# Tile-by-tile masks before the first attention, two count accumulators, and a head's sums copied between exponents in a graph network on one Trainium2 core

## The chip, the cores and the metric

One NeuronCore of a Trainium2 chip runs the whole program as one launch. The metric is the device time of that launch in microseconds; lower is better. Time before: 4402.19 us, the median of 3 runs (4397.08 to 4413.13).

The engines are TensorE (PE, its weight loads PEld), VectorE (DVE), ScalarE (ACT), GpSimd (POOL) and SyncE (SP, which only issues DMAs here). Each runs its own instruction stream in order; they meet through semaphores.

## The reference, cut to what matters

Four graph layers run over 1250 nodes with 768 features and 20000 edges, each followed by a residual and a layer norm:

1. three graph attentions of 4 heads with 192 features each (12 heads in all), then an output matmul;
2. a graph convolution normalised by degree;
3. an attention of 12 heads with 64 features each;
4. a relational convolution over 34 edge types, then a second graph convolution.

The part that the change touches is the attention: `e = leaky_relu(a_src[src] + a_dst[dst])`, `m = segment_max(e, dst)`, `p = exp(e - m[dst])`, `s = segment_sum(p, dst)`, `out = segment_sum(p / s[dst] * h[src], dst)`, and the count of edges between each pair of nodes on which the kernel bases it.

## The kernel before

**Dense counts.** Edges are sorted by destination tile (10 tiles of 128 nodes) and cut into BG = 49 groups of 512. For each group, VectorE makes one-hot matrices (`dve_compare`, lines 751 to 757), TensorE multiplies them (`pe_group`, L774) into a PSUM region `counted` of 1314 columns (banks 4 to 6), and VectorE adds that to the count table `ct` (`dve_add`, L765). Group k's product waits for addition k - 1 (`s_cta` at k + 2, which starts at 2), so product and addition alternate on the one region. The first 20 groups go two by two with the tiles of a dense product; the 29 others are a loop of their own.

**Phase 3.** After the last addition, VectorE computes `inv` (L792, L793), the inverse counts by relation, and then for each of 10 tiles: ScalarE copies a count row to f32 (`row`, L829), VectorE adds the identity (L802), writes `mask1` (L804, 0 where there is an edge or self loop, -1e30 elsewhere) and the second attention's mask over `ct` (L805), and sums the row into `deg` (L806). TensorE transposes the row (L822) and ScalarE copies it into `cnt` (L833). ScalarE then takes the root of the degrees (L848), and all five engines meet (`meet`, L167: each drains, adds one to a semaphore and waits for all).

**Attention** (class `Attention`, used twice: `att0` for the 12 wide heads, `att2` for the 12 narrow ones). A unit q = 10 h + s is a head h and a source tile s. Its parts:

- `maximum(t)` (DVE, L1027) takes the masked maximum of one destination tile of a head; ten make a head's, and `shifts(h)` (L1038 to L1049) turns them into three bf16 parts of a shift c, with the semaphore `s_c`. SP stores them to `shift_d` by an element-wise strided DMA (L963), waits for it, and loads them as a row `crow` (L968).
- ScalarE writes `relu` (L1182) of a unit in three pieces into PSUM banks 0 to 2, TensorE adds the shift (`add`, L1112), and ScalarE takes the exponent (L1191) of each piece into SBUF.
- `weigh(q)` (DVE, L1054) multiplies the exponents by the counts; `total(q)` (PE, L1139 narrow, L1150 wide) multiplies them by the features and accumulates over the ten units of a head.
- `prime` work: three one-row matmuls (L1159) that open banks 0 to 2.
- In `att2`, ScalarE copies a head's sums out of PSUM in three banks (`sums_out`, L1200), TensorE turns them back (L1123), and VectorE divides (`evict`, L1068 to L1071).

VectorE takes AHEAD + 10 = 20 maxima before its first `weigh`, and one more after each. `add(q + 2)` is issued inside `total(q)`. In `att2` the copies of head h - 1 stand at the end of ScalarE's work on unit 10 h + 1, after the relus of unit 10 h + 2; they wait for the semaphore `s_agg`, which only the third bank's matmul of a unit raises. `total(10 h)` may not overwrite bank k of the sums before copy k is done (`s_flat`).

## Time and profile before

| what | value |
|---|---|
| median of 3 runs | 4402.19 us (4397.08 to 4413.13) |
| the profiled execution | 4392.1 us, span 4390.5 us |
| PE / PEld busy | 3893.2 us (89%) / 2974.4 us (68%) |
| DVE / ACT / POOL busy | 2024.6 (46%) / 1552.3 (35%) / 1536.1 us (35%) |
| mean granted clock | 0.933 |

A busy share is a mean over stages with different limits, so each stage is read by itself. Times in rows are microseconds from the span's start; a mean "ns" is of one instruction; "idle before" is what the engine waited just before a group, with the releaser. The granted clock is TensorE's: 1.00 is 2.4 GHz, 0.50 is 1.2 GHz.

### The profile page before, as it was taken

The page shows a single profiled execution, that of the slowest core. Times are in us where ns is not written, and L with a number is a line of the kernel's source. Part 1 is how long each engine was busy: PE and PEld are TensorE (multiplying, and loading weights), DVE is VectorE, ACT ScalarE, POOL GpSimd, SP SyncE. Part 2 cuts the span into 40 slices and gives each one's busy share as a digit, 9 for nine tenths or more (in the row PEclk, how much of TensorE's full clock was granted, in tenths as well). Part 3 has the DMA queues.
Part 4 walks back from the last instruction along what each step waited for, and adds up shares of the span by engine and source line. Part 5 has one row for each costly group of instructions (what it writes and reads, how often), then busy time and mean ns, then how long its engine had stood idle before and what let it go on. Part 6 is the DMA issues. An engine that isn't in the chain of part 4 may idle for free. (4 is left out here: it accounts for less than half of the span.)

```text
span 4390.5 us, 57679 instructions
## 1 busy us (share of the span) xinstructions
PE 3893.2 (89%) x18441; PEld 2974.4 (68%) x18453; DVE 2024.6 (46%) x2795; ACT 1552.3 (35%) x2608; POOL 1536.1 (35%) x1191
## 2 busy tenths in 40 slices
PE   8998655999997869849999899999999999989979
PEld 4554324776767869722222389999999999965579
DVE  6337877666633343477877333322233322012224
ACT  1111014666662312137878323333333333300021
POOL 4888831444430000101111134444444444346600
PEclk9999876999998879978989899999999999999989
DMA  4342102343323231232212245555555554368821
GB/s 133 102 113 51 13 5 63 63 87 61 55 46 107 82 107 52 87 103 40 54 36 42 82 140 179 181 194 184 176 178 176 187 193 136 111 216 268 261 82 64
DMA packets 296918, 495.26 MB, mean 113 GB/s; under 512 B 159297, under 2 KB 175704, under 8 KB 296807
## 3 DMA queue, kind: packets, MB, share of 16 engines
q1 hardware_dynamic: 208678, 218.04, 17.2%
q0 software_dynamic: 53568, 181.40, 14.5%
q10 hardware_dynamic: 34560, 94.45, 6.1%
q8 instruction: 56, 0.92, 0.1%
q14 instruction: 56, 0.45, 0.0%
HBM read 365.96 MB, written 127.48 MB: 112 GB/s over the span
## 5 line engine op out<-in xcount | busy, mean ns | idle before, releaser
L1751 PE MATMUL ps<-wsplit,xsplit 128*128 x6840 | 1235.6, 337 | 1.3 <-POOL xsplit L1718 1.3
L1751 PEld LDWEIGHTS ps<-wsplit,xsplit 128*128 128x128 f32 x6840 | 1180.1, 188 | 1.5 <-issue 1.5
L1191 ACT ACTIVATE work<-ps,work 128x418 f32<-128x418 f32 x720 | 435.5, 606 | 357.2 <-PE ps L1112 336.5
L1054 DVE SCALAR_TENSOR_TENSOR work<-work,cnt 128x1250 f32<-128x1250 f32 x240 | 367.9, 1533 | 338.5 <-ACT work L1191 305.0
L1150 PE MATMUL ps<-hbuf,work 128*128 128x193 f32 x2400 | 497.6, 346 | 13.2 <-DVE work L1071 13.2
L1718 POOL TENSOR_TENSOR xsplit<-ct,xsplit 128x768 fp32r<-128x768 f32 x190 | 369.0, 1942 | 298.3 <-ACTq L1783 298.2
L1688 DVE CAST wsplit<-wplain 128x768 fp32r<-128x768 f32 x204 | 114.6, 562 | 760.9 <-PE ps L1751 742.4
L1150 PEld LDWEIGHTS ps<-hbuf,work 128*128 128x128 f32 x2400 | 387.8, 192 | 83.8 <-issue 83.8
L1182 ACT ACTIVATE ps<-work,lr 128x418 f32<-128x418 f32 x720 | 417.7, 605 | 23.5 <-DMA work<-lrow_d 23.5
L1788 ACT ACTIVATE ct<-ps,invs 128x768 f32<-128x768 f32 x190 | 171.5, 903 | 710.3 <-PE ps L1751 710.3
L1139 PE MATMUL ps<-work,hbuf 128*65 128x512 f32 x720 | 374.3, 606 | 37.5 <-ACT work L1200 27.5
L1713 POOL DMA_INDIRECT ct<-x_d,relrec x190 | 198.5, 1045 | 516.2 <-PE ps L1739 496.1
L1112 PEld LDWEIGHTS ps<-work 3*128 3x128 bf16 x720 | 65.6, 91 | 452.0 <-issue 200.9
L270 PE MATMUL ps<-wsplit,xsplit 128*128 128x384 f32 x1800 | 348.7, 354 | 12.8 <-DVE xsplit L402 12.8
L270 PEld LDWEIGHTS ps<-wsplit,xsplit 128*128 128x128 f32 x1800 | 335.7, 202 | 14.6 <-DVE xsplit L402 14.6
L1112 PE MATMUL ps<-work 3*128 3x418 bf16 x720 | 259.0, 361 | 90.8 <-DMA work<-shift_d 76.2
L1844 PE MATMUL ps<-work 128*128 128x384 f32 x784 | 267.2, 503 | 35.0 <-DVE work L1862 19.1
L1228 POOL DMA_INDIRECT invs<-inv_d,relrec x190 | 234.6, 1235 | 140.1 <-DVEq L167 82.5
L1844 PEld LDWEIGHTS ps<-work 128*128 128x128 f32 x784 | 152.9, 196 | 149.0 <-issue 34.1
L1689 DVE TENSOR_TENSOR wsplit<-wplain,wsplit 128x768 fp32r<-128x768 f32 x204 | 245.9, 1206 | 7.1
L722 POOL DMA_INDIRECT dstrec_d<-work x160 | 206.2, 1289 | 97.7 <-DVEq L646 49.3
L722 POOL DMA_INDIRECT relrec_d<-work x160 | 214.5, 1341 | 48.8 <-issue 48.8
(207 smaller groups left out, 4286.0 us busy)
## 6 DMA issues: line engine op xcount, KB each, us to landing
wplain<-in_L_gnn_W_rel SPq DMA_DIRECT2D x34, 2304.0 KB, 9.5
msg_d<-ct ACTq DMA_DIRECT2D x190, 384.0 KB, 2.6
work<-lrow_d SPq DMA_DIRECT2D x48, 625.0 KB
feat_d<-work ACTq DMA_DIRECT2D x30, 386.0 KB
hbuf<-feat_d SPq DMA_DIRECT2D x12, 965.0 KB
gat_d<-work POOLq DMA_DIRECT2D x12, 960.0 KB
xplain<-gat_d SPq DMA_DIRECT2D x30, 384.0 KB
work<-xa_d SPq DMA_DIRECT2D x27, 384.0 KB
```

The lines of the kernel that those rows point to most:

```text
L270: last = pe.matmul(o, x[:, u, c * P:(c + 1) * P], w[:, c * D + h * HALF:c * D + (h + 1) * HALF], start=(q == 0 and c == 0), stop=(q == 2 a ...
L722: g.indirect_dma_start(out=(relrec_d, dstrec_d)[which], out_offset=bass.IndirectOffsetOnAxis(addr[:, which, t:t + 1], 0), in_=(relpay[:, t ...
L1054: v.scalar_tensor_tensor(p[:, 0:N], p[:, 0:N], 1.0, cnt3[:, q % NT, 0:N], ALU.min, ALU.mult).then_inc(self.s_p, 1)
L1112: pe.matmul(ps[:, b, 0:c1 - c0], self.ones3, self.crow[h % 2][:, c0:c1], start=False, stop=True, skip_group_check=True).then_inc(self.s_ad ...
L1139: last = pe.matmul(ps[0:C + 1, 3 + k, 0:n1 - n0], self.feat(h, s), p[:, n0:n1], start=(s == 0), stop=(s == NT - 1))
L1150: last = pe.matmul(ps[:, self.b0 + b, t * (C + 1):(t + 1) * (C + 1)], p[:, dt * P:(dt + 1) * P], self.feat(h, s), start=(s == 0 and t == 0 ...
L1182: act.activation(ps[:, b, 0:c1 - c0], self.Rb[h % 2][:, c0:c1], ACT.Relu, bias=lr[:, col:col + 1]).then_inc(self.s_relu, 1)
L1191: act.activation(self.p[q % 3][:, c0:c1], ps[:, b, 0:c1 - c0], ACT.Exp, bias=self.l2[:, col:col + 1], scale=1.0 - SLOPE)\
L1689: step(v.tensor_tensor(wlo7[:, at:at + D], w, whi7[:, at:at + D].bitcast(F32), ALU.subtract))
L1718: g.tensor_tensor(xlo7[:, k % XW, :], xt7[:, k % 2].rearrange("p c n -> p (c n)"), xhi7[:, k % XW, :].bitcast(F32), ALU.subtract).then_inc ...
L1751: last = pe.matmul(ps[:, 4 + 2 * (u % 2) + h, 0:HALF], x[:, u, c * P:(c + 1) * P], w[:, bass.ds(base + (c * D + h * HALF), HALF)], start=( ...
L1844: last = pe.matmul(ps[:, 2 * (u % 2) + h, 0:HALF], sel8[:, GT * (u % 2) + w, :], mg8[:, GT * u + w, h * HALF:(h + 1) * HALF], start=(w == ...
```

## The change

- **Counting.** From the 22nd group on, the products go by turns to two PSUM regions (`counted` is now a list: banks 4 to 6, and 0 to 2), and group k's product waits only for addition k - 2. The attention's row transposes (`pe_lr_rows`) move up behind the 21st group's product.
- **Phase 3.** The degrees come from the 34 relation counts in one reduction of 340 elements; the root is taken after the first row. The masks become `dve_mask`, called tile by tile inside the attention's first ten maxima; the second attention's masks (`dve_mask2`) move into the third output product of `dve_wout`. The transposes go to `turned_ps`, PSUM columns from bank 3 on (2 x 1280), with an extra wait before the last two of a tile, since both tiles share a bank. The meeting between phase 3 and the first attention is gone; single waits take its place, and SP loads the attention's rows during counting (`before()` holds the waits that the features need).
- **Attention.** AHEAD is 4 (14 maxima before the first `weigh`), and each unit takes up to two more maxima until the lead is 20 again. The first head's shift (of both attentions) is transposed on TensorE, copied by ScalarE, and stored as 30 rows of 128 bf16. In `att2`, `sums_out` is split: bank k's copy stands behind exponent k of the unit, and waits for that bank's own matmul.

```diff
@@ pe_phase1
             W_H[2].multiply_single(pe, counts)
-            with pe.Fori(0, (BG - WITH_TILE * NT) // 2) as i:
-                for u in range(2):
-                    pe_group(pe, 2 * i + WITH_TILE * NT + u, u)
...
+            first = WITH_TILE * NT
+            pe_group(pe, first, 0)
+            pe.wait_ge(s_hread, 2 + 3 * NT)
+            pe_lr_rows(pe, 1)
+            pe.wait_ge(W_H[2].emptied, W_H[2].b["emptied"] + NT + 2)
+            with pe.Fori(0, (BG - 1 - first) // 2) as i:
+                for u in (1, 0):
+                    pe_group(pe, 2 * i + first + 2 - u, u, alternate=True)
...
-        counted = psf[:, 4 * 512:4 * 512 + CW]
+        counted = [psf[:, b * 512:b * 512 + CW] for b in (4, 0)]
...
-            pe.wait_ge(s_cta, k + 2)
+            pe.wait_ge(s_cta, k + (1 if alternate else 2))
+            sums = counted[u if alternate else 0]
@@ dve_phase3
             step(v.reciprocal(inv, inv))
             v.sem_inc(s_inv, 1)
+            step(v.tensor_reduce(deg, ct3[:, :, NP:CW], AX, ALU.add))
+            step(v.tensor_scalar(deg, deg, 1.0, None, ALU.add))
+            v.sem_inc(s_deg, 1)
             v.sem_inc(s_rused, 2)
...
+        def dve_mask(v, step, j):
+            row = crow[:, j % 2, :]
+            v.wait_ge(s_row, j + 1)
+            dg = row[:, j * P:(j + 1) * P]
+            step(v.tensor_tensor(dg, dg, ident[:, :], ALU.add))
+            v.sem_inc(s_crow, 1)
+            step(v.tensor_scalar(mask1[:, j * NP:(j + 1) * NP], row, 0.0, NONE, ALU.is_equal, ALU.mult))
+            v.sem_inc(s_rused, 1)
+
+        def dve_mask2(v, step, j):
+            c = ct[:, j * CW:j * CW + NP]
+            step.count(v.tensor_scalar(c.bitcast(BF16), c, 0.0, NONE, ALU.is_equal, ALU.mult))
@@ pe_phase3
-            pe_lr_rows(pe, 1)
+            pe.wait_ge(s_cta, 2 + BG)
+            att0.prime(pe)
...
-                    for s in range(NT):
-                        last = pe.transpose(psf[:, u * 2048 + s * P:u * 2048 + (s + 1) * P], crow[:, u, s * P:(s + 1) * P], ident[:, :])
+                    for k, s in enumerate((0, 1, 2, 3, 4, 5, 6, 7, 8, 9) if u == 0 else (2, 3, 4, 5, 6, 7, 8, 9, 0, 1)):
+                        if k == 8:
+                            pe.wait_ge(s_cout, j + 2)
+                        last = pe.transpose(turned_ps[u][:, s * P:(s + 1) * P], crow[:, u, s * P:(s + 1) * P], ident[:, :])
@@ Attention
-            AHEAD = NT
+            AHEAD = 4
...
+                def first_shift():
+                    sp.wait_ge(first_turned[1], self.turn)
+                    sp.dma_start(shift_d[0].rearrange("t (j p) -> (t j) p", p=P), self.turned).then_inc(self.s_c_out, 16)
+                    sp.wait_ge(self.s_c_out, self.at["c_out"] + 16)
+                    sp.dma_start(self.crow[0], shift_d[0]).then_inc(self.s_c_in[0], 16)
...
                 l_row(0)
+                r_row(0)
                 l_row(1)
-                r_row(0)
+                before()
                 features(0)
                 features(1)
-                shift(0)
+                first_shift()
                 l_row(2)
                 shift(1)
...
                 for t in range(NT + self.AHEAD):
+                    if t < NT:
+                        before(t)
                     maximum(t)
+                taken = NT + self.AHEAD
                 late = 3 if self.narrow else 0
                 for q in range(NT * H):
                     weigh(q)
-                    maximum(q + NT + self.AHEAD)
+                    upto = min(taken + 2, q + 1 + 2 * NT)
+                    for t in range(taken, upto):
+                        maximum(t)
+                    taken = upto
...
-                            if k == 2:
-                                last.then_inc(self.s_agg, 1)
+                            last.then_inc(self.s_agg, 1)
...
+                pe.wait_ge(self.s_c, self.at["c"] + 1)
+                pe.transpose(ps[0:3 * NT, 7, 448:512].bitcast(BF16), self.parts[0], self.ident).then_inc(first_turned[0], 1)
...
-                def sums_out(h):
-                    act.wait_ge(self.s_agg, self.at["agg"] + NT * (h + 1))
-                    if h:
+                def sums_out(h, k):
+                    if k == 0 and h:
                         act.wait_ge(self.s_back, h)
...
+                    act.wait_ge(self.s_agg, self.at["agg"] + 3 * (NT * (h + 1) - 1) + k + 1)
...
+                act.wait_ge(first_turned[0], self.turn)
+                act.activation(self.turned, ps[0:3 * NT, 7, 448:512].bitcast(BF16), ACT.Copy).then_inc(first_turned[1], 1)
                 for q in range(NT * H):
+                    turn = self.narrow and q >= NT and q % NT == 1
                     exponent(q, 0)
+                    if turn:
+                        sums_out(q // NT - 1, 0)
                     exponent(q, 1)
                     relu(q + 1, 0)
+                    if turn:
+                        sums_out(q // NT - 1, 1)
                     exponent(q, 2)
+                    if turn:
+                        sums_out(q // NT - 1, 2)
                     relu(q + 1, 1)
                     relu(q + 1, 2)
-                    if self.narrow and q >= NT and q % NT == 1:
-                        sums_out(q // NT - 1)
...
@@ the engines' programs
             dve_phase3(v, step)
-            meet(v)
-            att0.dve(v, step)
+            v.wait_ge(s_recs, 32)
+            for u in range(2):
+                v.wait_ge(s_h[u], 16 * (3 * NT // 2 + 1))
+            att0.dve(v, step, lambda j: dve_mask(v, step, j))
```

In the second attention `prime` now runs before the attention's own start on TensorE. Every engine's meeting before `att0` is removed in the same way; SP waits for the inverse counts' store only after the attention, GpSimd waits for it before its gathers.

## Rows read from the trace of the kernel before

**Rows 1.** The page: busy time, share of the span and instructions by engine

```profile
PE 3893.2 (89%) x18441; PEld 2974.4 (68%) x18453; DVE 2024.6 (46%) x2795; ACT 1552.3 (35%) x2608; POOL 1536.1 (35%) x1191
```

**Rows 2.** Stretches: width, busy time by engine, granted clock, DMA share, GB/s

```profile
487.17:638.26 151.09, 89.08 (x349) 36.92 (x350) 123.87 (x197) 0.38 (x1) 89.49 (x70) 0.83 0.06 3
638.26:725.10 86.84, 32.17 (x112) 22.34 (x112) 65.97 (x104) 32.27 (x34) 19.70 (x16) 0.51 0.28 56
725.10:1325.00 599.90, 572.52 (x2755) 419.86 (x2754) 357.06 (x473) 396.75 (x710) 225.99 (x185) 0.98 0.34 61
```

**Rows 3.** Groups by line, 487 to 639 us, and VectorE's last count addition

```profile
L765 DVE TENSOR_TENSOR ct<-ps,ct 128x1314 f32 x29 | 44.1, 1519 | 12.7 <-PE ps L774 12.2 <-issue 0.4
...
636.73 1.53 DVE L765 TENSOR_TENSOR ct<-ps,ct 128x1314 f32 x1 [2.69 <-PE ps L774]
```

**Rows 4.** Timeline, 638 to 681 us: start, duration, engine, idle before

```profile
638.79 2.28 DVE L793 RECIPROCAL work<-work 128x340 f32<-128x340 f32 x1
...
646.26 0.29 DVE L802 TENSOR_TENSOR work<-work,ident 128x128 f32 x1 [0.34 <-DVE work L806]
...
646.79 0.83 DVE L804 TENSOR_SCALAR mask<-work 128x1280 f32 x1 [0.24 <-DVE work L802]
646.83 1.27 ACT L829 ACTIVATE work<-ct 128x1280 f32 x1
...
647.94 1.48 DVE L806 TENSOR_REDUCE work<-work 128x1280 f32 x1
...
679.47 1.28 ACT L848 ACT_TABLE_LOAD   x1
```

**Rows 5.** Timeline, 685 to 724 us: the first attention's way to its first unit

```profile
687.37 1.46 DVE L1027 CUSTOM_DVE_ANT_0 work<-mask,work 128x1250 f32<-128x1250 bf16 x1 [0.19 <-DVE work L1027]
...
703.55 0.37 SPq L963 DMA_DIRECT2D shift_d<-work  x1
...
718.34 0.27 SPq L968 DMA_DIRECT2D work<-shift_d  x1
...
723.54 1.46 DVE L1054 SCALAR_TENSOR_TENSOR work<-work,cnt 128x1250 f32<-128x1250 f32 x1 [2.18 <-ACT work L1191]
```

**Rows 6.** Timeline, 1935 to 1978 us: the second attention's shift and weights

```profile
1935.53 0.37 SPq L963 DMA_DIRECT2D shift_d<-work  x1
...
1956.07 1.46 DVE L1054 SCALAR_TENSOR_TENSOR work<-work,cnt 128x1250 f32<-128x1250 f32 x1 [2.32 <-ACT work L1191]
1977.46 1.46 DVE L1054 SCALAR_TENSOR_TENSOR work<-work,cnt 128x1250 f32<-128x1250 f32 x1 [0.57 <-ACT work L1191]
```

**Rows 7.** Stretches from one L1200 start to the next, columns as in 2

```profile
2037.91:2084.75 46.84, 44.11 (x100) 10.56 (x100) 33.52 (x54) 33.77 (x65) 5.53 (x3) 0.78 0.24 42
...
2126.07:2165.04 38.97, 35.04 (x100) 9.13 (x100) 35.01 (x54) 33.44 (x64) 5.53 (x3) 1.00 0.24 51
...
sum 465.94, PE 430.23 PEld 106.48 DVE 339.06 ACT 361.79 POOL 61.02; mean PE 39.11 PEld 9.68 DVE 30.82 ACT 32.89 POOL 5.55
```

**Rows 8.** TensorE's waits, 1960 to 2450 us: total, times, longest

```profile
PE ps L1139 <- ACT work L1200: 27.5, 11, 2.5
```

**Rows 9.** One-microsecond stretches around a gap of TensorE, columns as in 2

```profile
2083.00:2084.00 1.00, 0.00 (x0) 0.00 (x0) 1.00 (x2) 1.00 (x3) 0.00 (x0) 1.00 0.77 3
...
2086.00:2087.00 1.00, 1.00 (x2) 0.00 (x0) 1.00 (x2) 0.08 (x1) 0.00 (x0) 0.50 0.43 1
```

**Rows 10.** Timeline of one unit of the second attention at full clock

```profile
2066.45 1.46 DVE L1054 SCALAR_TENSOR_TENSOR work<-work,cnt 128x1250 f32<-128x1250 f32 x1 [0.57 <-ACT work L1191]
...
2067.38 0.60 ACT L1191 ACTIVATE work<-ps,work 128x418 f32<-128x418 f32 x1
...
2068.95 1.07 PE L1139 MATMUL ps<-work,hbuf 128*65 128x512 f32 x2
...
2069.87 1.46 DVE L1054 SCALAR_TENSOR_TENSOR work<-work,cnt 128x1250 f32<-128x1250 f32 x1 [0.57 <-ACT work L1191]
```

**Rows 11.** Groups by line, 2126.07 to 2165.04 us: busy, mean ns, idle before

```profile
L1054 DVE SCALAR_TENSOR_TENSOR work<-work,cnt 128x1250 f32<-128x1250 f32 x11 | 18.3, 1663 | 3.6 <-ACT work L1191 3.4
```

More of the change, by code:

```diff
@@ L773, in pe_group @@
                     n1 = min(n0 + 512, CW)
[L774 removed]
+                    last = pe.matmul(sums[:, n0:n1], oh_t[:, GT * u + w, :], oh_s[:, GT * u + w, n0:n1],
                                      start=(w == 0), stop=(w == GT - 1))
@@ L779, in build @@
         c3 = Carve(work, WORK)
+        c3(4 * KC * D)
+        turned_ps = [psf[:, 3 * 512 + u * NP:3 * 512 + (u + 1) * NP] for u in range(2)]
         crow = c3(2 * NP).rearrange("p (u n) -> p u n", u=2)
@@ L1167, in pe, with prime @@
                     turn_back(H - 1)
+            def prime(self, pe):
+                for b in range(3):
+                    pe.matmul(ps[:, b, :], ones[0:1, :], ident[0:1, :].unsqueeze(1).to_broadcast([1, 4, P]), start=True, stop=True)\
+                      .then_inc(self.s_primed, 1)
             def act(self, act):
```

89 lines of the change are left out of this document (39 added, 50 removed).

## The prediction

> **What bounds the kernel now.** I read the page first: TensorE is busy for 89% of the span [rows 1], so a change can only help where TensorE waits or runs at its lower clock. Then the stretches around the edited code. In the counting loop, 487 to 638 us, TensorE is busy 89.1 us of 151 and VectorE 123.9: VectorE bounds it [rows 2]. From the last count addition to the first attention's products, 86.8 us, TensorE does 32 us of work at a granted clock of 0.51 (1.2 GHz): a chain of VectorE, ScalarE and DMAs bounds it. In the first attention itself TensorE is busy 572.5 us of 599.9 at 0.98; nothing there is to be had. Last the second attention. I cut it at the starts of the sum copies (L1200), which gives 11 stretches of one head. They take 465.9 us, 42.4 us a head, and the only one at a clock of 1.00 throughout takes 38.97 [rows 7]. Who waits for whom gives the first reason: TensorE waits 11 times, 27.5 us in all, 2.5 each, for those copies [rows 8]. One-microsecond stretches give the second: TensorE's gap is followed by a fall of the granted clock from 1.00 to 0.50 [rows 9].
>
> **The change, part by part. Counting.** Before the additions of this loop VectorE waits 12.2 us for TensorE, 2.69 of it before the last [rows 3]. With two regions, product k runs while VectorE adds k - 1, so these waits vanish. TensorE has room even at the low clock (89.1 of 151 us busy [rows 2]), and each product's one-hots are ready before the addition that precedes its own. Bounds: 0 (TensorE becomes the bound) and 12.2; I take 12.2, since VectorE is the busier by 35 us. The row transposes placed behind group 20 cost TensorE under 1 us, in that room. Gain 12.2.
>
> **From the last addition to the first weigh.** Before: the addition ends at 636.73 + 1.53 = 638.26 [rows 3], the first `weigh` starts at 723.54 [rows 5]: 85.3 us. After, counted from that end:
> - `inv`: the reciprocal ends at 638.79 + 2.28, that is 2.8 [rows 4]. The new reduction has 340 elements where L806 takes 1.48 us for 1280; I take 0.4 (bounds 0.2 and 1.48), with a small addition and waits to 3.8.
> - the first row's copy, 1.27 [rows 4]: 5.1. VectorE meanwhile does the attention's small preparations.
> - ten tiles on VectorE, each identity addition 0.29, mask 0.83 [rows 4], maximum 1.46 [rows 5], and gaps of 0.1 to 0.2: 3.0 a tile (bounds 2.7 and 3.4). L805 and L806 no longer stand in a tile. 35.1.
> - the arithmetic of the shift. From the second maximum at 687.37, nine maxima of 1.46 + 0.19 end at 702.2, and the store is issued at 703.55 [rows 5]: 1.4. 36.5.
> - ScalarE copies the last turned tile (as 1.27) and does three relus (as the 0.60 in rows 10), done at about 38.1, then copies the turned shift: 38.4.
> - the store of 30 rows. No row shows such a one. From above it is the element-wise store, 718.34 - 703.55 = 14.8 us; from below the load that follows it: load to first weigh is 5.2 [rows 5], of which an addition and three exponents take 2.2 to 2.7, so a DMA of this size takes 2 to 3. It is nearest to the load: 2.1. 40.5.
> - load, addition, exponents as before, 5.2: 45.7.
>
> So 85.3 - 45.7 = 39.6 us. The ScalarE and TensorE side of a tile (two copies of 1.27, and the last two transposes that wait for the neighbour's copy) comes to some 2.75 us a tile by my count and hides behind VectorE's 3.0; if it doesn't, each 0.1 us costs 1. SP: the attention's rows are loaded during counting; the inverse counts' store stands ahead of the features, but both come earlier than today's meeting. GpSimd's gathers start when that store lands, earlier too. The four further maxima, 6.6 us, fit into the 7.8 us of the shift's way.
>
> The root is moved between row 0 and row 1, with its table load of 1.28 us [rows 4]: row 1 is ready at 5.1 + 1.5 + 1.27 = 7.9, and VectorE comes to tile 1 at 8.1, so it costs nothing. The Trainium skill, "ScalarE: Activation LUTs", section "What ACT_TABLE_LOAD costs", adds a drain of about 1.38 us to each load; by it row 1 would come 1.2 us after VectorE asks, once. The row shows the load straight behind the copy before it, and the sum keeps the 1.28.
>
> **The shorter lead.** VectorE takes two maxima a unit until it is 20 ahead: six units of about 4.5 us (three instructions of 1.46 and a gap). In the first attention a unit lasts 5.0 us (120 in 599.9 [rows 2]), so only the shift's arithmetic in the third unit shows: loss 1.4 (bounds 0 and 5). In the second, the shift's store is issued at 1935.53 and the first weigh starts at 1956.07 [rows 6], 20.5 us later; with turn and copy 1.0, store 2.1, and 5.6 for the load to the weigh, plus 0.4 of waits, it is 9.1: gain 11.4. But its units last 3.42 [rows 10]: six of 4.5 and 1.8 of shift are 28.8 us where the first six took 21.4 [rows 6]: loss 7.4. Net 4.0 (bounds -3 and 11).
>
> **The head's sums.** At full clock [rows 10], measured from a weigh's start at 2066.45: ScalarE's next exponent runs from 0.93 to 1.53, and the product of the first bank starts at 2.50. A copy as long as an exponent (0.60) put behind it ends at 2.1, so TensorE no longer waits. The products of the other banks follow 1.3 us apart, and their copies, each behind an exponent, end some 0.2 to 0.7 ahead of them. ScalarE's unit becomes 1.3 us longer where it had 0.2 of slack; the weigh comes 0.7 later, which the 1.0 us between the end of a weigh and its product absorbs. I leave 0.2 us a head (bounds 0 and 1). The head at full clock, 38.97 [rows 7], becomes 36.7. VectorE allows it: it waits 3.6 of those 38.97 us [rows 11], so its floor is 35.4. And with no gap of this size left, the clock should stay at 1.00 as in that head. 42.4 - 36.7 = 5.7 us, 11 times: 62.7.
>
> **At nothing:** the second attention's masks in the output product (ten instructions, each at most the 0.83 of a mask; VectorE waits there for products; 8 us if the cover were gone), the reciprocal of the roots (0.2), the priming.
>
> Sum: 12.2 + 39.6 - 1.4 + 4.0 + 62.7 = 117.1. The profiled execution's own time is 4392.1, and 4392.1 - 117.1 = 4275.0; the median of the runs shown stands 10.1 above that execution, so 4285.
>
> **Rivals.**
> - *The clock falls anyway.* TensorE still has short waits in a head, and ScalarE's burden of copies may make one more. Of the measured excess only 2.5 - 0.2 us a head would go, 25 us in all, 37 less: 4322. For it: only one head of 11 kept its clock. Against: rows 9 show the fall right behind the gap that goes away. Chance 0.15.
> - *The catch-up starves TensorE.* In the second attention it idles about 1.1 us of each 4.5 for six units, which may hold the clock at 0.50. The load of head 1's row also stands on SP behind the second, element-wise shift store (14.8 us), which now starts in unit 3; by my count it lands 2 us before it is needed. 15 us: 4300. Chance 0.12.
> - *The new store is as slow as the old one* (bound above): 12.7 us twice: 4310. Chance 0.05.
> - *Slower:* the double maxima and the copies thin TensorE's work so that the second attention stays at 1.2 GHz. Rows 7 give the price: 46.84 us at 0.78 against 38.97 at 1.00, 0.76 us per microsecond of full clock lost, so a head all at 0.50 takes 63. Eleven of those, less the 2.3 us of waits, lose 200 where the rest gains 54: 4548. It decides once a head takes over 47.3 us, a mean clock of some 0.76. Against: every head before recovers its clock. Chance 0.02.
> - *The parts don't add up,* another transfer or wait ends last in two places and less than a fifth is left: about 4385. Chance 0.04.
>
> The forecast has 0.62, with 4270 to 4300 as its own range. The range 4265 to 4325 takes in the bounds of the tiles, the lead and the copies, the clock's fall and the slow store. Half a per cent, 22 us, is about what a measurement of this kernel can tell from no change: faster by more 0.95, within it 0.03, slower 0.02.
>
> **What would show it.** Right: no idle before the count additions; 45.7 us from the last addition to the first weigh; the first shift's load issued within 3 us of its store; L1200 to L1200 about 36.7 us at a clock of 1.00; no wait of TensorE for L1200. Wrong: a clock at 0.50 behind the head changes; VectorE waiting for rows or for ScalarE in the mask tiles; ScalarE waiting for a loaded row in unit 9; VectorE idle before masks in the output product's stage replaced by TensorE waiting for VectorE.

## The result, and the profile after

The kernel after takes 4261.74 us (median; 4258.26 to 4286.96) against 4407.66 (4397.08 to 4425.16) before: ratio 0.9676, 95% interval 0.9634 to 0.9719. The forecast was 4285 with a range from 4265, so the kernel is faster by more than was forecast and ends 3 us outside the range. The profiled execution is the slowest of the runs: 4286.96 us, span 4285.4, while the one before stood 10 us under the median stated for it at the start. That matters below.

The page's first part, and then two stretches of the kernel after (width, busy time by engine, granted clock, DMA share, GB/s), against [rows 1, 2]:

```profile
PE 3856.1 (90%) x18430; PEld 2972.0 (69%) x18455; DVE 2010.9 (47%) x2789; ACT 1547.3 (36%) x2610; POOL 1546.5 (36%) x1191
```

```profile
625.81:670.80 44.99, 28.69 (x114) 19.69 (x114) 37.95 (x69) 32.31 (x35) 30.99 (x16) 0.59 0.26 63
670.80:1295.30 624.50, 582.62 (x2753) 427.20 (x2754) 363.92 (x485) 396.56 (x710) 219.46 (x186) 0.96 0.34 59
```

The way into the first attention went from 86.8 us to 45.0. The first attention itself, from its first to its last product of a head's sums, went from 597.0 us (725.1 to 1322.1 in the kernel before) to 624.5, at a lower clock: here the profiled execution gave 27.5 us back.

Counting and the way to the first weighing, by groups and by timeline, against [rows 3 to 5]:

```profile
L770 DVE TENSOR_TENSOR ct<-ps,ct 128x1314 f32 x30 | 45.4, 1514 | 2.3 <-PE ps L782 1.3 <-issue 1.1
```

```profile
624.28 1.53 DVE L770 TENSOR_TENSOR ct<-ps,ct 128x1314 f32 x1 [1.05 <-issue]
```

```profile
628.76 0.51 DVE L805 TENSOR_REDUCE work<-ct 128x10 f32<-128x340 uint16 x1
...
629.75 1.27 ACT L848 ACTIVATE work<-ct 128x1280 f32<-128x1280 uint16 x1 [138.54 <-DVEq L808]
...
631.04 1.28 ACT L860 ACT_TABLE_LOAD   x1
...
663.45 0.36 SPq L978 DMA_DIRECT2D shift_d<-work  x1
...
664.84 0.26 SPq L980 DMA_DIRECT2D work<-shift_d  x1
...
669.15 1.46 DVE L1086 SCALAR_TENSOR_TENSOR work<-work,cnt 128x1250 f32<-128x1250 f32 x1 [0.61 <-ACT work L1234]
```

The wait of the additions for TensorE is 1.3 us in all where it was 12.2. The last addition ends at 625.81, the first weighing starts at 669.15: 43.3 us. The store of 30 rows has landed 1.4 us after its issue (the element-wise one took 14.8).

The second attention: first its shift's store and first weighing, against [rows 6], then stretches of a head, now from one L1244 to the next, against [rows 7], then TensorE's waits from 1961 to 2359 us, against [rows 8]:

```profile
1912.48 0.34 SPq L978 DMA_DIRECT2D shift_d<-work  x1
...
1918.18 1.45 DVE L1086 SCALAR_TENSOR_TENSOR work<-work,cnt 128x1250 f32<-128x1250 f32 x1
```

```profile
1997.93:2034.59 36.66, 35.06 (x102) 9.13 (x101) 35.11 (x52) 33.01 (x65) 5.53 (x3) 1.00 0.29 54
...
2291.16:2326.14 34.98, 34.84 (x102) 9.11 (x101) 19.89 (x25) 32.91 (x64) 5.54 (x3) 1.00 0.27 38
2326.14:2358.80 32.66, 32.58 (x96) 8.96 (x96) 15.65 (x14) 27.84 (x55) 5.53 (x3) 1.00 0.09 21
sum 396.83, PE 382.62 PEld 100.20 DVE 344.86 ACT 358.38 POOL 62.11; mean PE 34.78 PEld 9.11 DVE 31.35 ACT 32.58 POOL 5.65
```

```profile
PE ps L1178 <- DVE work L1086: 13.3, 26, 0.9
```

All eleven heads run at a clock of 1.00, and TensorE's wait for the copies is gone from the list. The 11 stretches take 396.8 us instead of 465.9.

**Where the 105.1 us between the two spans lie** (before less after, at the same milestones; 4390.5 less 4285.4):

| stretch | before | after | gain |
|---|---|---|---|
| end of the last count addition | 638.26 | 625.81 | 12.4 |
| from there to the first weighing | 85.3 | 43.3 | 41.9 |
| first attention, first to last product | 597.0 | 624.5 | -27.5 |
| from there to the second attention's first maximum | 595.2 | 598.3 | -3.1 |
| first maximum to first copy of a head's sums | 78.2 | 68.4 | 9.8 |
| 11 heads, first copy to last | 465.9 | 396.8 | 69.1 |
| last copy to the end | 1929.1 | 1926.6 | 2.5 |

One border in this table moves with the change itself. In the kernel before the first copy stands behind the relus of its unit and starts 0.4 us after that unit's weighing starts; in the kernel after it stands behind the first exponent and starts 2.8 us ahead of the weighing. So part of the 9.8 us belongs to the copies; the first experiment says how much.

**The first attention's heads.** Cut at VectorE's first instruction of each eviction, a head is either short or long. Two neighbours in the kernel after:

```profile
719.77:779.36 59.59, 51.44 (x230) 37.35 (x230) 32.41 (x45) 33.43 (x61) 18.36 (x17) 0.89 0.34 56
779.36:827.71 48.35, 47.16 (x230) 34.49 (x230) 32.40 (x44) 33.62 (x61) 21.49 (x17) 1.00 0.41 68
```

The kernel before has two long heads (57.0 and 58.7), the kernel after five (59.6, 58.1, 58.5, 55.1, 57.4); all others take 48.4 in both, but for the last stretch, 45.5. So a run's time depends on how many long heads it happens to get.

### The profile page after: what moved, and what is told of

The parts are those of the page before. It is cut to its first block and busy times, and to the rows that moved or that the text cites. A ratio compares the mean times of both kernels' runs of the same rounds, so it can differ in the third digit from the quotient of the medians.

```text
span 4285.4 us, 57585 instructions
## 1 busy us (share of the span) xinstructions
PE 3856.1 (90%) x18430; PEld 2972.0 (69%) x18455; DVE 2010.9 (47%) x2789; ACT 1547.3 (36%) x2610; POOL 1546.5 (36%) x1191
## 5 line engine op out<-in xcount | busy, mean ns | idle before, releaser
L1188 PE MATMUL ps<-hbuf,work 128*128 128x193 f32 x2400 | 505.9, 351 | 13.2 <-DVE work L1103 13.1
L1178 PE MATMUL ps<-work,hbuf 128*65 128x512 f32 x720 | 339.1, 554 | 17.0 <-DVE work L1086 16.1
L1889 POOL DMA_INDIRECT work<-msg_d,work x196 | 195.3, 997 | 104.6 <-issue 55.8
```

Of the source, the lines that this page charges most:

```text
L1178: last = pe.matmul(ps[0:C + 1, 3 + k, 0:n1 - n0], self.feat(h, s), p[:, n0:n1], start=(s == 0), stop=(s == NT - 1))
L1188: last = pe.matmul(ps[:, self.b0 + b, t * (C + 1):(t + 1) * (C + 1)], p[:, dt * P:(dt + 1) * P], self.feat(h, s), start=(s == 0 and t == 0 ...
```

## The experiments

They were run in six groups, each on one chip together with the kernel before, whose medians there were 4403 (first group), 4401, 4386, 4426, 4356 and 4386 us. Groups 3 and 4 ran on the same chip, and yet the kernel before differs by 40 us between them. So a time is to be read with its ratio to the kernel before of its own group and, for small effects, with the trace. "Long" counts first-attention heads of over 53 us, of the eleven stretches between evictions (the head ahead of the first eviction isn't among them); "1st" is its length from first to last product.

| kernel | group | us | ratio, 95% | 1st | long |
|---|---|---|---|---|---|
| b_split_sums | 1 | 4324.3 | 0.9813 (0.9738-0.9889) | 607.9 | 3 |
| b_filled_wait | 1 | 4355.9 | 0.9891 (0.9853-0.9929) | 626.6 | 4 |
| a_whole_sums | 1 | 4324.3 | 0.9802 (0.9730-0.9875) | 614.0 | 3 |
| a_again | 1 | 4263.2 | 0.9668 (0.9602-0.9733) | 605.0 | 3 |
| a_bank_evict | 2 | 4281.9 | 0.9731 (0.9693-0.9769) | 627.4 | 5 |
| a_ahead_ten | 2 | 4277.0 | 0.9724 (0.9679-0.9770) | 600.3 | 2 |
| a_slow_shift | 2 | 4283.9 | 0.9732 (0.9687-0.9777) | 613.5 | 3 |
| a_one_region | 2 | 4279.8 | 0.9720 (0.9675-0.9765) | 615.2 | 3 |
| a_spread_loads | 3 | 4251.0 | 0.9697 (0.9660-0.9734) | 591.6 | 1 |
| a_few_features | 3 | 4246.3 | 0.9682 (0.9646-0.9718) | 591.8 | 2 |
| a_gathers_later | 3 | 4234.3 | 0.9655 (0.9625-0.9686) | 577.6 | 0 |
| a_masks_first | 3 | 4259.8 | 0.9710 (0.9678-0.9741) | 588.9 | 1 |
| b_gathers_later | 4 | 4382.9 | 0.9910 (0.9876-0.9943) | 577.7 | 0 |
| a_later_and_banks | 4 | 4220.2 | 0.9532 (0.9497-0.9568) | 561.9 | 0 |
| a_gathers_apart | 5 | 4216.9 | 0.9681 (0.9662-0.9701) | 577.7 | 0 |
| a_third | 6 | 4259.0 | 0.9706 (0.9671-0.9742) | 608.2 | 3 |
| b_gathers_apart | 6 | 4381.2 | 0.9995 (0.9969-1.0022) | 579.9 | 0 |
| a_apart_and_banks | 6 | 4224.9 | 0.9634 (0.9602-0.9667) | 563.4 | 0 |

### The head's sums: what is the wait, what the clock

b_split_sums makes this part of the change alone in the kernel before:

```
+                last.then_inc(self.s_agg, 1)        # for each bank, not k == 2 alone
+                if turn: sums_out(q // NT - 1, k)   # k = 0, 1, 2, behind exponent k
-                sums_out(q // NT - 1)               # behind the unit
...
```

> The kernel before, with only the copies of a head's sums put between the exponents of the second unit of the next head (and TensorE's count of products made per bank); nothing else of the change. Theory A (the whole gain of the second attention is the copies'): the 11 heads from first copy to first copy, 465.9 us in the kernel before, take about 397 us as in the kernel after, TensorE's wait for the copies (27.5 us in all) is under 6 us, and the time falls by 62 to 70 us. Theory B (part of the gain is due to the maxima that are now taken in pairs behind a lead of four tiles): the heads stay above 405 us here and the time falls by under 55 us.

Its 11 heads take 396.4 us (after: 396.8), all at 1.00. And from the first maximum to the first copy it takes 75.2 us where the kernel before took 78.2. The second attention from its first maximum to its last copy, before and in this kernel (columns as in [rows 2]):

```profile
1917.27:2461.41 544.14, 469.07 (x1190) 115.76 (x1190) 404.53 (x562) 402.86 (x754) 61.02 (x33) 0.86 0.21 42
```

```profile
1925.82:2397.47 471.65, 420.40 (x1187) 109.16 (x1188) 407.50 (x562) 396.34 (x755) 62.10 (x33) 0.95 0.24 48
```

So the copies are worth 72.5 us: 69.5 in the 11 stretches and 3.0 in front of the first copy. The time fell by 79 us by the medians, more than the 62 to 70 expected; the kernel before scatters by over 60 us in that group. Theory A holds: the heads' whole gain is the copies'.

b_filled_wait fills the wait instead of removing it:

```
 if s == 0 and h and k == 0:
+    ...                                       # from h = 2 on, a wait for s_free
+    for _ in range(12):
+        pe.matmul(ps[:, 7, 384:512], ident[:, :], ident[:, :], start=True, stop=True, ...)
 pe.wait_ge(self.s_flat, ...)
```

> The kernel before, with 12 products of the identity with itself (128 columns, fp32) put into TensorE's queue ahead of its wait for a head's copied sums; they go to columns that nothing reads and change no result, and the copies stay where they were. Theory A (of the 5.7 us by which a head was to become shorter, about 3.4 us is the price of the clock that falls behind the wait, and 2.3 to 2.5 us the wait itself): the granted clock of the second attention goes from 0.85 to 0.95 or more, a head goes from 42.4 us to about 39 us, and the time falls by 30 to 40 us. Rival B (the clock falls whatever fills the wait, or the whole price is the wait): heads stay at 42 us or more, clock at 0.85, time within 8 us of before. Rival C (the wait costs nothing beyond the clock): heads reach 36.7 us, the time falls by more than 55 us.

Stretches of its heads, L1206 to L1206:

```profile
2102.87:2142.25 39.38, 38.02 (x129) 12.16 (x128) 33.88 (x44) 33.43 (x64) 5.53 (x3) 1.00 0.25 50
...
sum 424.57, PE 410.94 PEld 128.54 DVE 341.28 ACT 359.90 POOL 62.12; mean PE 37.36 PEld 11.69 DVE 31.03 ACT 32.72 POOL 5.65
```

Every head keeps its full clock though the copies are as late as ever. 465.9 - 424.6 = 41.4 us is the price of the clock, 3.8 a head; 424.6 - 396.4 = 28.1 us, 2.6 a head, that of the wait. The split is a little rough, for the twelve products run on past the first copy:

```profile
2101.54 2.94 PE L1141 MATMUL ps<-ident 128*128 128x128 f32 x24 [0.45 <-DVE work L1054]
2102.87 1.33 ACT L1206 ACTIVATE work<-ps 65x512 f32<-65x512 f32 x3
2104.32 1.02 PE L1145 MATMUL ps<-work,hbuf 128*65 128x512 f32 x2
```

Its full heads take 39.4 us where the one undisturbed head of the kernel before took 38.97 [rows 7], so the clock's price is rather above 3.8 and the wait's rather below 2.6. The median is 48 us under the kernel before (30 to 40 were expected), with four long heads in the trace. So idling made the clock fall, as [rows 9] suggested, and it cost more than the wait itself: theory A.

a_whole_sums undoes this part in the kernel after (each of the three copies behind the unit, waiting for the whole).

> The kernel after, with the three copies put back behind the second unit of the next head, each waiting for the whole of the sums. Theory A: heads go back from 36.1 us to about 42.4 us each, the granted clock of the second attention from 0.94 to about 0.85, and the time rises by 62 to 70 us over the kernel after, so that this kernel takes 4324 to 4332 us. Theory B (the other parts took away some of the stall too): a rise of under 50 us.

The heads take 451.6 us, 54.8 more than in the kernel after, and the time rises by 61 us over a_again, just under the 62 to 70 of theory A. It is less than in b_split_sums, since these heads lost less clock than those of the kernel before (mean 0.92 against 0.88; one at 1.00, the slowest 48.3 us at 0.75). Without this part of the change the heads themselves scatter, from 38.7 to 48.3 us.

### The ways into the two attentions

a_one_region: `sums = counted[0]` and `pe.wait_ge(s_cta, k + 2)` for all groups.

> The kernel after, with the products of all groups counted into one region again, so that a group's products wait for the addition of the group before. Theory A (the alternation is worth 12 us): the last addition of the counts ends about 12 us later, at 636 to 638 us instead of 624.3 and 624.7, and all behind it moves along: 4272 to 4278 us by the median. Theory B (the alternation gains nothing, and the 12 us come from the lr rows being turned earlier): 0 to 2 us.

The last addition starts at 635.9 instead of 624.0 to 624.7 in three traces of the kernel after: some 11.5 us, nearly all of the counting's gain, so theory A. The ratio is 0.4% above that of the kernel after, which the intervals alone don't tell from nothing.

a_slow_shift: `shift(0)` in place of `first_shift()`, without the turn and its copy.

> The kernel after, with the first shift of each attention stored element by element from its parts, as in the kernel before, instead of turned by TensorE and copied by ScalarE to rows first. Theory A (that store takes 14.8 us against 1.4 us, and the turn and the copy cost 1.3 us): the first weighing comes about 12 us later in each attention, and the time is 4283 to 4292 us by the median. Theory B (the new way's gain is hidden behind the maxima in the lead): 7 us or less each.

From the last addition's start to the first weighing it takes 58.5 us instead of 44.9 (13.6 more, 12 expected); from the second attention's first maximum to its first copy 88.6 instead of 67.2, which is 21.4 and not 12. There the first weighing comes 14.4 us later, and the first head behind it takes 49.6 us instead of 42.6 up to its copy. These last 7 us weren't forecast; in that stretch the mean clock is 0.71 where a_again has 0.86. Theory A holds, at a higher price.

a_ahead_ten: `AHEAD = NT`.

> The kernel after, with the lead of the maxima at ten tiles of the second head, as in the kernel before, instead of four. Theory A (VectorE's maxima stand between the shift's landing and the first weighing: six more at 1.46 us and their read of 0.08 us, less what now hides behind the shift's way): in both attentions the first weighing comes about 8 us later, in all 4272 to 4282 us by the median. In the first attention addition to first weighing goes from 44.9 to about 53 us, in the second from the first maximum to the first copy of sums from 67.2 to about 75 us. Theory B (the shift's way through memory ends last and hides them): under 2 us each, time within 5 us of the kernel after.

It takes 55.5 instead of 44.9 us in the first attention (10.6 more) and 81.5 instead of 67.2 in the second (14.3 more): theory A, with a price above the 8 expected.

a_masks_first: all ten masks, then the maxima.

> The kernel after, with the masks of all ten tiles taken before the maxima of the first head instead of tile by tile between them. Theory A (in the kernel after a tile takes 2.95 us, in which the maximum fills VectorE's wait for the next row from ScalarE; ahead of them all the masks would still take about 2.2 us each by ScalarE's row and copy, and the ten maxima of 1.55 us follow): the first weighing comes about 8 to 15 us later, addition to first weighing 53 to 60 us against 44.9. Theory B (ScalarE bounds the tiles and the maxima of the lead run while the shift is on its way anyway): less than 5 us.

It takes 56.1 us instead of 44.9, 11.2 more: theory A. Its tiles without a maximum still take 2.3 to 2.7 us each (once 3.7), for VectorE now waits 0.9 to 1.4 us in most of them for ScalarE's row. In the change the maxima fill that wait. Its median is no worse than the kernel after had in group 1, but it has one long head where three traces of the kernel after have 3 to 5: seen by the time alone, the loss would have been missed.

### Why a head of the first attention is long or short

a_again and a_third are the kernel after, unchanged.

> The kernel after, unchanged, for a second trace of it. In its first trace the first attention, from first to last product of the head sums, took 624.5 us at a mean granted clock of 0.955, against 597.0 us at 0.98 in the kernel before. Theory A (the clock of the first attention falls at some head changes in some executions and not in others; nothing of the change makes it longer): this trace shows another length, between 595 and 625 us, which goes with its granted clock, and a time that lies 25 us lower has its 25 us there. Theory B (the change itself makes the first attention longer, by its maxima in pairs or by work that was moved into it): it is again 620 to 628 us, and what makes other executions shorter lies elsewhere.

> The kernel after, unchanged, on the chip of the next two. Its ratio to the kernel before is again 0.963 to 0.972. In its trace each long head of the first attention (54 us or more) costs 6 to 13 us over 48.4, and all of the difference between its first attention and 577.6 us is in such heads.

605.0 and 608.2 us, with three long heads each, against 624.5 with five. Theory A holds: the change doesn't make the first attention longer, the number of long heads does. My first reason for them was the stand of TensorE at each head change, as its waits show it (kernel after, 670 to 1295 us):

```profile
PE ps L1188 <- DVE work L1103: 13.1, 11, 1.2
```

a_bank_evict takes it away:

```
-    v.wait_ge(self.s_agg, self.at["agg"] + NT * (h + 1))
+    for b in range(5):                        # s_bank: by the last product of banks 0 to 3
+        v.wait_ge(s_bank, 4 * h + b + 1)      # bank 4: s_agg
+        (sum + TINY, reciprocal and product of this bank)
```

> The kernel after, with VectorE taking a head of the first attention out of its five banks one by one: it waits for the last product of each bank instead of the last of all, so bank 0 is free before TensorE starts the next head. In six traces a head of the first attention takes either 48.4 us at a granted clock of 1.00 or 54.5 to 61.6 us with a clock of 0.88 to 0.94; how many of its heads are of the second kind (2 in the kernel before, 5 and 3 in two traces of the kernel after) makes up all the difference in its length. Theory A (the clock falls some 20 to 26 us behind a head change because TensorE stood for 1.2 us there): without the stand all heads take 47.2 us, the first attention from first to last product 563 to 575 us against 605.0 and 624.5, no head is at a clock below 0.97, and the time is 4216 to 4232 us, with less scatter between runs. Theory B (falls come whatever TensorE does at a head change): only the stands go, 11 times 1.2 = 13 us, heads of 57 us stay, the time is 4243 to 4255 us.

The stands are gone from its trace (46.9 us for a short head instead of 48.4), but five heads take 57 to 63 us. Theory A misses: the long heads were to vanish. The trace is B's, but B's 13 us don't show in the time, for the ratio came out 0.5% over the kernel after's. So the stand is not what makes the clock fall here. (The next expectation speaks of six long heads in this kernel; they are five.)

What a long head looks like, in ScalarE's timeline of the kernel after, in one-microsecond stretches, and as ScalarE's waits in the first attention:

```profile
740.70 0.61 ACT L1234 ACTIVATE work<-ps,work 128x418 f32<-128x418 f32 x1 [2.68 <-PE ps L1151]
744.22 0.61 ACT L1234 ACTIVATE work<-ps,work 128x416 f32<-128x416 f32 x1 [2.91 <-remote]
744.73 0.60 ACT L1225 ACTIVATE ps<-work,lr 128x418 f32<-128x418 f32 x1
749.20 0.61 ACT L1234 ACTIVATE work<-ps,work 128x416 f32<-128x416 f32 x1 [3.87 <-remote]
```

```profile
740.00:741.00 1.00, 0.85 (x6) 0.55 (x4) 0.00 (x0) 0.30 (x1) 0.69 (x2) 1.00 1.12 315
741.00:742.00 1.00, 0.00 (x0) 0.00 (x0) 0.00 (x0) 0.31 (x1) 0.92 (x1) 1.00 0.52 125
742.00:743.00 1.00, 0.00 (x0) 0.00 (x0) 0.00 (x0) 0.00 (x0) 0.77 (x1) 0.95 0.02 1
743.00:744.00 1.00, 0.00 (x0) 0.00 (x0) 0.00 (x0) 0.00 (x0) 0.69 (x2) 0.50 0.01 0
```

```profile
ACT work L1234 <- remote: 32.3, 10, 4.8
```

The exponent at 744.22 needs an addition that TensorE started at 737.54, the one at 749.20 an addition started at 739.00 and 0.34 long. ScalarE stands for no reason that the profile names ("remote"), TensorE runs dry at 741, and only then does the clock go to 0.50. (Below, a load is a DMA that SP issues for a coming head, and a gather is one that GpSimd issues by a list of rows.) What else goes on: a burst of loads from SP (733 to 742 us, up to 349 GB/s), and GpSimd's gathers of inverse counts, 16 a head, of which the timeline shows one every 1.3 to 2.5 us, right behind GpSimd's own store of the last head's 960 KB output. In short heads all of these are there too. Three kernels take them apart: the features in five pieces behind units 4 to 8 and the r row behind unit 5; nine of twelve loads of features left out; and the gathers moved:

```
-    att0.pool(g, lambda h: gather_inverses(g, 16 * h, min(RT, 16 * (h + 1))))
+    att0.pool(g)
-    att2.pool_rows(g, step)
+    att2.pool_rows(g, step, lambda h: gather_inverses(g, 18 * h, min(RT, 18 * (h + 1))))
```

> The kernel after, with a head's loads in the first attention taken apart: the l row as before, the r row after the 5th unit of the head, the features in five pieces after units 4, 6, 7, 8 and 8, instead of all of them within 1.2 us of the queue. What the nine traces so far show: every head of the first attention that takes 54 us or more has stands of ScalarE of 2 to 8 us in front of an exponent whose products were added long before, which begin while these loads run (733 to 742 us in the kernel after), and the granted clock falls only behind them; the stand of TensorE at the head change is there in all heads, also in those of 48.4 us, and a kernel without it had six long heads. Theory C (the loads in one burst cause the stands): with the loads apart no head is above 50 us, no clock below 0.97, the first attention from first to last product is 577 to 582 us, against 605.0 and 624.5 in two traces of the kernel after, and the time is 4232 to 4243 us with little scatter. Rival D (the stands have to do with another thing that runs at that time: the gathers of inverse counts, or nothing that the kernel moves): long heads stay, time within 8 us of the kernel after.

> The kernel after, with the features of only the first three heads of the first attention loaded (the other nine heads use these again, so their sums are of other features); the l and r rows are loaded as before. 9 of 12 loads of 965 KB are left out, of 2.2 MB per head. Theory C (the burst of loads causes ScalarE's stands): fewer or no long heads from the third on; the first attention is 577 to 590 us. Rival D: 2 to 5 long heads as before, time within 10 us of the kernel after.

> The kernel after, with the 190 gathers of inverse counts, which GpSimd issues 16 to a head in the first attention, moved to the second attention (18 to a head, ahead of the rows that GpSimd works on there). Theory D1 (the gathers, which end at about the time of ScalarE's stands, have a part in them): no long heads in the first attention, 577 to 582 us; the second attention may get them instead. Theory C (the loads alone): 2 to 5 long heads as before, first attention 597 to 627 us, time within 10 us of the kernel after.

With the gathers elsewhere the first attention has no long head, and in four runs the time stays within 6 us (4230.4 to 4236.5). In the list of ScalarE's waits in the first attention there is no line with "remote" left, and the heads of the second, which now has the gathers, stay at 395.8 us. With the loads apart one long head stays, with the loads thinned two, and single runs still reach 4283 and 4262 us. Alone these two kernels show little of the loads' part, since a_masks_first and a_ahead_ten, which leave the loads alone, also have just one and two. But the long head of a_spread_loads is telling. The only transfer that SP issued in it ahead of the stands is one row of 625 KB, and the DMA engines' time from 731 to 737 us, when the first stand begins, went more to GpSimd's queue (q0: gathers and store) than to SP's (q1):

```profile
734.09 0.33 SPq L959 DMA_DIRECT2D work<-lrow_d  x1
739.15 0.61 ACT L1238 ACTIVATE work<-ps,work 128x416 f32<-128x416 f32 x1 [2.88 <-remote]
```

```profile
q0 software_dynamic: 305, 0.69, 46.2%
q1 hardware_dynamic: 116, 0.55, 30.8%
```

So a large burst from SP isn't needed, and a store of GpSimd's own goes on beside it. a_gathers_apart keeps the gathers in the first attention, behind the loads and behind that store:

```
+    def apart(h):
+        if h: g.wait_ge(att0.s_agg, NT * h + 6)
+        gather_inverses(g, 16 * h, min(RT, 16 * (h + 1)))
```

> The kernel after, with GpSimd waiting for the sixth unit of a head before it issues the head's 16 gathers of inverse counts, so that they run behind the head's loads (which end in the fifth unit) instead of beside them; the first head's 16 stay where they were. Theory E (a stand needs loads and gathers in the same microseconds): no long head from the second on, the first attention from first to last product 577 to 590 us (the first heads may still meet), time 4232 to 4245 us. Theory F (gathers alone make ScalarE stand): long heads in 1 to 5 of 11, with the stands now in the second half of a head, time within 10 us of the kernel after.

ScalarE's waits in it, and one head's stretch with its gathers in it:

```profile
ACT work L1234 <- PE ps L1151: 173.8, 353, 1.6
```

```profile
720.00:768.40 48.40, 47.20 (x231) 34.49 (x230) 32.40 (x44) 33.66 (x61) 16.08 (x13) 1.00 0.41 69
```

Theory E: no long head, and a scatter of 12 us. So gathers alone didn't make ScalarE stand here, and loads alone didn't either (a_gathers_later): it took both in the same microseconds. Whether SP's loads or GpSimd's store matters beside the gathers isn't shown, for this edit takes the gathers away from both. It also moves them from the first half of a head to the second, and no run tells that apart. Its 4216.9 us don't compare with other groups, since the kernel before took 4356 on that chip, and from the last copy to the end this kernel took 1901.8 us where every other trace has 1924.5 to 1930.5. The ratio, 0.9681, is no better than that of the kernel after. So the removal of long heads is shown by the traces and the smaller scatter, not by that group's ratio.

### Both kernels without long heads, and a better version

> The kernel before, with the 190 gathers of inverse counts moved from the first to the second attention, as it was done with the kernel after, which then took 4234 us. Theory A (the long heads of the first attention come of these gathers in both kernels, and the change itself is worth what its milestones show, 12.4 in the counting, 42 up to the first weighing, 10 at the start of the second attention, 69 in its heads and 3 behind, 136 us in all): all heads of the first attention at 48.4 us, 577 to 578 us from first to last product, scatter under 10 us, time 4366 to 4374 us. Theory B (the sum of the forecast, 117 us, is the change's worth, and the rest was scatter): 4348 to 4355 us.

No long head, 577.7 us, as theory A has it; but the median, 4382.9, lies 9 us above its range, and the runs scatter by 23 us where under 10 were expected. The profiled executions stand at 4371.0 and, with the change, 4230.4: 140.6 us. That is above the 136 that I had added up, since in this kernel the first copy of sums comes 84.8 us after the second attention's first maximum where the kernel before took 78.2. Its clock there keeps falling, too. The medians, 4382.9 and 4234.3, are 148.6 apart, but stand in two groups between which the kernel before moved by 40 us, so this figure means little.

> The kernel before, with the gathers of inverse counts issued behind the sixth unit of a head. Theory A (long heads trouble both kernels): no long head, first attention 577 to 578 us, 10 to 25 us faster than the kernel before by the median; with the change's milestones worth 136 us, a kernel with the change and the same gathers lies some 130 to 150 us below it. Theory B (the gathers matter to the kernel after alone): time within 8 us of the kernel before.

Theory A misses in the time: the ratio is 0.9995. Its trace has no long head either (579.9 us; the 2.2 us more lie ahead of the first eviction, where its gathers still run beside the loads), yet its runs scatter from 4364 to 4408 us. The second attention's clock, which this kernel doesn't change, may give such a scatter, but one trace doesn't show it, nor how many long heads the other executions have. That the gathers cost the kernel before anything by its median is not shown.

> The kernel after, with the gathers in the second attention and a head of the first attention taken out of its banks one by one. With no long heads left, the 11 stands of TensorE of 1.2 us at the head changes (13.1 us) remain as the only ones. Theory A (TensorE sets the pace of the first attention, so they count in full): heads of 47.2 us, 564 to 566 us from first to last product against 577.6, time 4219 to 4224 us. Theory B (another engine catches up in the stand, so it is worth less): heads of 48 us or more, time above 4228 us.

> The kernel after, with the gathers behind the sixth unit and a head of the first attention taken out of its banks one by one. With the gathers in the second attention the banks gave heads of 47.1 us and 561.9 us from first to last product. The same here, no long head, and a time 30 to 50 us below the kernel after on this chip, with a scatter of under 15 us. If the ten more small instructions of VectorE per head bring the long heads back, it is within 20 us of the kernel after.

The first attention of a_later_and_banks (width, busy time, clock):

```profile
672.30:1234.20 561.90, 561.87 (x2755) 415.08 (x2754) 377.99 (x582) 397.57 (x710) 10.57 (x11) 1.00 0.38 65
```

TensorE shows no idle time (561.87 of 561.90 us), so no wait is left to remove in this stage. The edit that was worth nothing beside long heads is worth 15.7 us without them (577.6 to 561.9). Beside the kernel after on one chip, a_apart_and_banks takes 4224.9 us against 4259.0 (a_third): 34 us less, scatter 7 us against 24. Some 15 of these are the banks', so about 19 are left for the gathers; no group has the kernel after beside one with the gathers alone moved. a_later_and_banks has 4220.2 and 0.9532, in the group in which the kernel before was slowest.

## Why the forecast was too high

The mechanisms were the ones named, and no rival came true; sizes in the sum were too small. With the two kernels' long heads taken out (19.3 us over 577.7 before, 46.9 over 577.6 after), the spans differ by 105.1 + 27.6 = 132.7 us, where the forecast has 117.1. Point by point:

- *Counting*, 12.2: measured 12.4; undone alone, 11.5.
- *Last addition to first weigh*, 45.7: measured 43.3. The tiles take 2.95 us (3.0 forecast); the store 1.4 us instead of 2.1 (and under the 2 to 3 read off the load), load to weigh 4.3 instead of 5.2, the new reduction 0.51 instead of 0.4. (The 7.8 us that the forecast gives for the shift's way are 9.2 by its own list, 36.5 to 45.7; the four maxima fit in, for VectorE waits another 0.61 us before the first weighing.) The sum kept the plain 1.28 us for the table load: it starts at 631.04, 0.02 us behind the end of the copy (629.75 + 1.27). Of the drain of 1.38 us, which the Trainium skill ("ScalarE: Activation LUTs", "What ACT_TABLE_LOAD costs") adds, this place shows nothing.
- *The shorter lead in the first attention*, -1.4: without long heads the first attention is as long as before (577.6 and 577.7), so 0.
- *The shorter lead and the new store in the second*, 4.0: measured 6.8, which is the table's 9.8 less the 3.0 that b_split_sums shows to be the copies'. The shift's way is 6.4 us (1911.8 to 1918.18) instead of 9.1; it brings the first weighing 14.2 us nearer to the first maximum (24.6 for 38.8), 2.8 more than the 11.4 forecast. The slower start behind it came as forecast: the first ten units take 43.9 us for 36.3, a loss of 7.6 (6.4 and 6.5 in the other two traces of the kernel after), where the sum has 7.4. Its first six units took 28.7 us at a mean clock of 0.72.
- *The head's sums*, 62.7: measured 72.1, that is 69.1 in the 11 stretches and 3.0 ahead of them (72.5 in b_split_sums). Nine heads take 36.0 to 36.7, as forecast. The last two take 35.0 and 32.7: they have few or no maxima, and the last holds 96 instructions of TensorE for the others' 102. I had carried the full-clock head with all its maxima over to all eleven, and left out that the first copy, too, now comes earlier.
- *At nothing*: the masks, the root and the priming cost nothing that shows. The two stretches outside the attentions gave -3.1 and 2.5 us together, within what other traces of the kernel after show (594 to 598 for the first).

The step that failed is the sizing of the sum, above all the term "the head's sums": 62.7 us, where the runs show 72. The second attention's start adds 2.8, the way to the first weighing 2.4 and the lead in the first attention 1.4: with the small ones 15.6 us in all.

A second step failed behind the sum: the 10.1 us added for the median. 4392.1 - 132.7 = 4259.4, and the median is 2.3 above that, so the rest of the 23.3 us by which 4285 was too high, some 7.7, comes from there. The 10.1 belonged to one execution, which had two long heads and its own falls of the clock in the second attention; in the kernel after this offset is -25.2, with five long heads in the profiled execution. The forecast had no term for long heads. That 4259.4 lies so near to the median is in part luck, for it takes the 19.3 us of long heads of one execution before as those of the usual execution after, whose three traces have 27 to 47.

The line on the first attention, "nothing there is to be had", was wrong too: the clock of 0.98 in [rows 2] hid two heads of 57.0 and 58.7 us among the short ones, and 13.2 us of stands at the head changes (13.1 in the kernel after).

## What to carry to other kernels

Cut a long uniform stage into its periods before you call it full: equal periods with a few long ones mean a chance event, and a mean clock of 0.98 hides it. Before a profiled time is set against a median, count such events in the profiled execution. And where a wait drops the clock, price both: in these traces filling the wait with products that nothing reads was worth 41 us, removing it 72.

## What the runs showed of the hardware

- A TensorE wait of 2.5 us at each head change cost at most 2.6 us itself and some 3.8 us by the clock behind it. The same wait filled with products that nothing reads left the clock at 1.00 in all 11 heads.
- The stands of TensorE of 1.2 us in the first attention, 11 in a run, leave the clock alone (10 heads of 48.4 us at 1.00 in a_gathers_later).
- ScalarE stood for 2 to 8 us in front of instructions whose producers were long done, when GpSimd's indirect gathers ran in the same microseconds as large transfers (SP's loads, GpSimd's own store). It did so in 1 to 5 of 11 heads in each of the 14 traces with the gathers there. In all six kernels that had the gathers behind these transfers or out of the stage, no long head was traced. Which of the transfers matters, and through what the gathers hold ScalarE up, stays open: no row shows the resource.
- On one of the chips the time from the last copy to the end was 1901.8 us where every other trace has 1924.5 to 1930.5, and on another the kernel before's median moved by 40 us between two groups. So times of different groups differ by more than small changes do.
